# Expert gate and up products of a routed feed-forward layer: one float32 product against three float32r products of halves made on chip

## The reference

```
logits = jnp.einsum('bsd,ed->bse', x, w_router)          # 8 experts
top_vals, top_idx = jax.lax.top_k(logits, 2)
rw = jax.nn.softmax(top_vals, axis=-1)
gate = jnp.einsum('bsd,efd->ebsf', x, w_gate)            # d = 256, f = 512
up = jnp.einsum('bsd,efd->ebsf', x, w_up)
h = jax.nn.silu(gate) * up
y = jnp.einsum('ebsf,edf->bsed', h, w_down)
out = sum over the two chosen experts of rw * y, then a layer norm
```

## Time and profile before

| what | value |
|---|---|
| three runs | 1172.77, 1178.34 and 1179.01 us, median 1178.34 us |
| the profiled execution | 1180.64 us, of which the span of instructions is 1178.8 us |
| instructions | 20227 |
| busy in the span | TensorE 88%, VectorE 61%, ScalarE 47%, GpSimd 51% |

### The profile page before, as it was taken

The page is one execution under the profiler, slowest core; times in us unless marked ns, Lnnn a source line. Parts: engine busy times, 40 slices in busy tenths (PEclk is TensorE's granted clock), DMA queues, the critical chain, the costliest instruction groups (busy, mean ns, idle before and its releaser), DMA issues.

```text
span 1178.8 us, 20227 instructions
## 1 busy us (share of the span) xinstructions
PE 1033.9 (88%) x5678; PEld 823.7 (70%) x5679; DVE 723.2 (61%) x1870; ACT 559.0 (47%) x1201; POOL 604.3 (51%) x662
## 2 busy tenths in 40 slices
PE   5878999999999999995997892799999999999920
PEld 4668999999999999984565662356666666666610
DVE  3766888888888888986778974122222222222237
ACT  1446877887788776651534540122222222222223
POOL 4524776687668767776145666133333333333346
PEclk8979999999999999997978965799999999999965
DMA  9442001001000000111534523122222222222263
GB/s 273 130 116 83 1 3 63 1 1 38 27 1 2 11 1 10 55 55 50 199 119 166 163 55 97 37 45 45 45 45 45 45 45 45 45 44 45 45 144 124
DMA packets 54737, 75.43 MB, mean 64 GB/s; under 512 B 9349, under 2 KB 46979, under 8 KB 52613
## 3 DMA queue, kind: packets, MB, share of 16 engines
q1 hardware_dynamic: 32392, 48.80, 13.3%
q0 software_dynamic: 16640, 18.50, 9.4%
q10 hardware_dynamic: 5628, 7.22, 2.2%
HBM read 45.35 MB, written 29.11 MB: 63 GB/s over the span
## 4 chain that ended last, share of the span: by engine, by line
PE 78%; DVE 6%; issue 5%; DMA 5%; SPq 2%; ACT 2%; POOL 2%; DVEq 0%; POOLq 0%; ACTq 0%
PE bank L1410 19%; PE bank L1149 17%; PE bank L1214 9%; PE bank L1426 9%; PE bank L1209 3%; PE bank L1418 2%; PE bank L1309 2%; PE bank L1119 2%; DMA arena_b<-in_patches 2%; PE bank L1197 2%; PE bank L1177 1%; PE bank L1185 1%; PE bank L1198 1%; SPq L504 1%; PE bank L1312 1%
## 5 line engine op out<-in xcount | busy, mean ns | idle before, releaser
L1077 POOL DMA_INDIRECT yrows<-arena_b,dest_i x64 | 99.8, 1559 | 270.7 <-ACT arena_b L900 258.8
L1410 PE MATMUL bank<-arena_a,arena_b 128*128 x512 | 235.6, 603 | 0.9 <-ACT arena_b L888 0.6
L1559 DVE SCALAR_TENSOR_TENSOR arena_b<-bank,sml,arena_b 128x304 f32<-128x304 f32 (+2 forms) x384 | 195.4, 522 | 23.5 <-ACT arena_b L732 20.3
L1886 DVE TENSOR_TENSOR arena_b<-bank,arena_b 128x512 f32<-128x512 f32 x64 | 44.2, 691 | 200.8 <-PE bank L1410 200.8
L1149 PE MATMUL bank<-xt_hi,w_hi 128*128 128x308 f32 x512 | 160.2, 313 | 1.8 <-DVE arena_b L1559 1.3
L1410 PEld LDWEIGHTS bank<-arena_a,arena_b 128*128 128x128 f32 x512 | 93.0, 192 | 98.4 <-issue 94.7
L1149 PE MATMUL bank<-xt_hi,w_lo 128*128 128x308 f32 x512 | 157.7, 308 | 0.0
L1149 PE MATMUL bank<-xt_lo,w_hi 128*128 128x308 f32 x512 | 156.9, 306 | 0.0
L979 POOL TENSOR_TENSOR u_halves<-arena_b,u_halves 128x308 fp32r<-128x308 f32 x128 | 110.1, 867 | 37.6 <-ACT arena_b L744 37.5
L973 POOL TENSOR_TENSOR y_lo<-arena_b,y_hi 128x308 fp32r<-128x308 f32 x128 | 108.1, 857 | 31.5 <-ACT y_hi L756 31.2
L1426 PE MATMUL bank<-arena_a,arena_b 128*128 x512 | 121.3, 380 | 1.4 <-DVE arena_b L1898 0.9
(11 more groups left out here) (179 smaller groups left out, 2210.4 us busy)
## 6 DMA issues: line engine op xcount, KB each, us to landing
arena_b<-xrows SPq DMA_DIRECT2D x64, 129.0 KB
arena_a<-in_w_gate SPq DMA_DIRECT2D x4, 1024.0 KB
arena_a<-in_w_up SPq DMA_DIRECT2D x4, 1024.0 KB
arena_a<-in_w_down SPq DMA_DIRECT2D x4, 1024.0 KB
yrows<-arena_b SPq DMA_DIRECT2D x1, 3648.0 KB, 18.6
h_all<-seq SPq DMA_DIRECT2D x8, 448.0 KB
w_raw<-in_w_in SPq DMA_DIRECT2D x3, 1024.0 KB
arena_a<-yrows SPq DMA_DIRECT2D x4, 448.0 KB
```

Source lines behind the costliest of these rows:

```text
L1077: pool.indirect_dma_start(yrows, bass.IndirectOffsetOnAxis(ap=dest_i[:, k:k + 1], axis=0), f_y[k], None, compute_op=ALU.add).then_inc(y_se ...
L1410: mm = pe.matmul(bank[q][:, :], x_gt[k][:, d, :], w[:, d, bass.ds(e * FFN, FFN)], start=(d == 0), stop=(d == DC - 1))
L1559: dve.scalar_tensor_tensor(acc[:, :, back_:TXT], x[:, :, 0:TXT - back_], conv_w(s // GROUPS, c, tap), acc[:, :, back_:TXT], ALU.mult, ALU. ...
```

## The change

The gate and up products are taken from halves. ScalarE makes the upper halves of the gate and up weights of block j+1's expert (`upper_weights`, two copies of 128x1024), VectorE the lower halves (`lower_weights`, two subtractions of 128x1024), both in the step of block j. The rows get halves too: ScalarE's copy out of bank 2 now writes `x_hi`, and VectorE subtracts it from bank 2 into `x_lo` (`lower_rows`, 128x256). TensorE then runs twelve float32r matmuls of 512 columns where four float32 matmuls were. ScalarE and VectorE read `expert_i` themselves; TensorE reads it in `down` alone. The two halves of each kind have two buffers, which lie over text memory that is free by then, and over `padbuf`; so ScalarE waits for the sends out of `padbuf` before its first copy. The last norm's small tensors move to another tile, with no other change.

```diff
             def turn(j, k):
                 act.wait_ge(f_tr, j + 1)
                 wait(act, f_um, j - 1)
-                act.activation(x_gt[k], bank[2][...], ACT.Copy).then_inc(f_trc, 1)
+                wait(act, f_xlo, j - 1)
+                act.activation(x_hi[k][:, :, :], bank[2][...], ACT.Copy).then_inc(f_trc, 1)
+            def upper_weights(j, k):
+                e = act.value_load(expert_i[0:1, bass.ds(j, 1)], min_val=0, max_val=EXPERTS - 1)
+                wait(act, f_um, j - 1)
+                wait(act, f_wul, j - 1)
+                act.activation(wg_hi[k][:, :, :], wg_s[:, :, bass.ds(e * FFN, FFN)], ACT.Copy).then_inc(f_wg, 1)
+                act.activation(wu_hi[k][:, :, :], wu_s[:, :, bass.ds(e * FFN, FFN)], ACT.Copy).then_inc(f_wu, 1)
             def expert_step(j, k):
+                upper_weights(j + 1, 1 - k)
                 gate(j)
                 turn(j + 1, 1 - k)
                 back_half(j - 1, 1 - k)
...
             def gate_up(j, k):
-                e = pe.value_load(expert_i[0:1, bass.ds(j, 1)], min_val=0, max_val=EXPERTS - 1)
-                pe.wait_ge(f_trc, j + 1)
-                for q, w, sig, free in ((0, wg_s, f_gm, f_silu), (1, wu_s, f_um, f_hh)):
+                pe.wait_ge(f_xlo, j + 1)
+                for q, hi, lo, ready, sig, free in ((0, wg_hi, wg_lo, f_wgl, f_gm, f_silu), (1, wu_hi, wu_lo, f_wul, f_um, f_hh)):
+                    pe.wait_ge(ready, j + 1)
                     wait(pe, free, j)
-                    for d in range(DC):
-                        mm = pe.matmul(bank[q][:, :], x_gt[k][:, d, :], w[:, d, bass.ds(e * FFN, FFN)], ...)
+                    pairs = [(x, w, d) for d in range(DC) for x, w in ((x_hi, hi), (x_hi, lo), (x_lo, hi))]
+                    for n_, (x, w, d) in enumerate(pairs):
+                        mm = pe.matmul(bank[q][:, :], x[k][:, d, :], w[k][:, d, :], ...)
                     mm.then_inc(sig, 1)
...
+            def lower_weights(j, k):
+                e = dve.value_load(expert_i[0:1, bass.ds(j, 1)], min_val=0, max_val=EXPERTS - 1)
+                dve.wait_ge(f_wg, j + 1)
+                wait(dve, f_um, j - 1)
+                dve.tensor_tensor(wg_lo[k][:, :, :], wg_s[:, :, bass.ds(e * FFN, FFN)], wg_hi[k][:, :, :].bitcast(F32), ALU.subtract)\
+                    .then_inc(f_wgl, 1)
+                dve.wait_ge(f_wu, j + 1)
+                dve.tensor_tensor(wu_lo[k][:, :, :], wu_s[:, :, bass.ds(e * FFN, FFN)], wu_hi[k][:, :, :].bitcast(F32), ALU.subtract)\
+                    .then_inc(f_wul, 1)
+            def lower_rows(j, k):
+                dve.wait_ge(f_trc, j + 1)
+                wait(dve, f_um, j - 1)
+                dve.tensor_tensor(x_lo[k][:, :, :], bank[2][...], x_hi[k][:, :, :].bitcast(F32), ALU.subtract).then_inc(f_xlo, 1)
+            def expert_step(j, k):
+                lower_weights(j + 1, 1 - k)
+                hidden(j, k)
+                lower_rows(j + 1, 1 - k)
+                destinations(j, k)
+                hidden_turned(j, k)
```

More of the change, by code:

```diff
@@ L218, in build, with expert_sb @@
         at = [0]
+        EXPERT_COLS = 2 * ROW + 4 * FFN + 2 * D + GB * 6 + GROUPS * GB * 6
+        with ExitStack() as expert_memory:
+            def expert_sb(name, shape, dt=F32R):
+                return expert_memory.enter_context(nc.sbuf_tensor(name, shape, dt))
+            expert_b = expert_sb("expert_b", [P, EXPERT_COLS], F32)
+            x_hi, x_lo, wg_hi, wg_lo = ([expert_sb(f"{name}{k}", [P, DC, cols]) for k in range(2)]
+                                        for name, cols in (("x_hi", P), ("x_lo", P), ("wg_hi", FFN), ("wg_lo", FFN)))
+            wu_hi = [expert_sb("wu_hi0", [P, DC, FFN])]
+        assert EXPERT_COLS + 4 * DC * P + 5 * DC * FFN <= 9856
         arena_b = sb("arena_b", [P, 9856])
@@ L295, in build @@
         h_all = sb("h_all", [SEQ, BATCH, D])
+        with ExitStack() as expert_memory:
+            wu_hi.append(expert_sb("wu_hi1", [P, DC, FFN]))
+            wu_lo = [expert_sb(f"wu_lo{k}", [P, DC, FFN]) for k in range(2)]
+        assert 3 * DC * FFN <= (EXPERTS + SPARE) * ROW
         padbuf = sb("padbuf", [P, EXPERTS + SPARE, ROW])
@@ L377, in build @@
         at[0] = 0
[L378 to L383, removed]
+        x_g = [part(expert_b, ROW) for _ in range(2)]
+        f_sg = part(expert_b, FFN)
+        f_h = part(expert_b, FFN)
+        f_ht = [part(expert_b, FFN).rearrange("p (c t) -> p c t", c=FC) for _ in range(2)]
+        f_y = [part(expert_b, D) for _ in range(2)]
         at[0] = 0
@@ L387, in build @@
         assert at[0] <= (DC * FFN * 2 + FC * D) * EXPERTS
[L388 to L391, removed]
+        at[0] = 2 * ROW + 4 * FFN + 2 * D
+        y_st = part(expert_b, GB * 6, rows=SEQ).rearrange("p (k s) -> p k s", k=GB)
+        y_mv = [part(expert_b, GB * 2, rows=SEQ).rearrange("p (k s) -> p k s", k=GB) for _ in range(GROUPS)]
+        y_rs = [part(expert_b, GB * 4, rows=SEQ).rearrange("p (s k) -> p s k", s=4) for _ in range(GROUPS)]
         bank = [ctx.enter_context(nc.psum_tensor(f"bank{k}", [P, 512], F32)) for k in range(8)]
@@ L887, in turn @@
                 wait(act, f_um, j - 1)
-                act.activation(x_gt[k], bank[2][:, 0:DC * P].rearrange("p (c t) -> p c t", c=DC), ACT.Copy)\
+                wait(act, f_xlo, j - 1)
+                act.activation(x_hi[k][:, :, :], bank[2][:, 0:DC * P].rearrange("p (c t) -> p c t", c=DC), ACT.Copy)\
                     .then_inc(f_trc, 1)
@@ L905, in expert_step @@
                 back_half(j - 1, 1 - k)
+            act.wait_ge(ld_ffn, 16 * len(FFN_PIECES))
             act.wait_ge(tbl_ready, 2)
+            act.wait_ge(pad_sent, 16 * EXPERTS)
+            act.wait_ge(spare_sent, 16)
+            for k in range(len(x_sent)):
+                act.wait_ge(x_sent[k], 16 * 2 * GB * (GROUPS // len(x_sent)))
+            upper_weights(0, 0)
             turn(0, 0)
+            upper_weights(1, 1)
             gate(0)
@@ L1398, in turn_block @@
                 pe.wait_ge(x_in[k], turn_ * 16 + 16)
-                wait(pe, f_trc, j)
+                wait(pe, f_xlo, j)
                 for d in range(DC):
@@ L1898, in hidden_turned @@
                 dve.tensor_copy(f_ht[k], bank[3][:, :].rearrange("p (c t) -> p c t", c=FC)).then_inc(f_htc, 1)
[L1900 to L1908, removed]
+            def expert_step(j, k):
[4 more added lines that the diff above has]
+                hidden_turned(j, k)
+            lower_weights(0, 0)
+            lower_rows(0, 0)
+            expert_step(0, 0)
+            expert_step(1, 1)
+            expert_step(2, 0)
+            with dve.Fori(1, BLOCKS // 2 - 1) as pair:
+                expert_step(pair * 2 + 1, 1)
+                expert_step(pair * 2 + 2, 0)
+            hidden(BLOCKS - 1, 1)
+            destinations(BLOCKS - 1, 1)
+            hidden_turned(BLOCKS - 1, 1)
             def row_gain(g):
```

7 lines of the change are left out of this document (5 added, 2 removed).

## The result

The changed kernel takes 1219.11 us in the median of 4 runs (1218.34 to 1228.22), beside 1178.38 (1172.77 to 1179.01, 4 runs) before: a ratio of 1.035, 95% interval 1.0306 to 1.0394. It is slower; 1162 had been forecast, with a range that ended at 1179. The profiled execution took 1218.34 us, its span is 1216.3 (1178.8 before).

What follows compares the result with a forecast made beforehand. TensorE was taken to bound the expert stage at 11.79 us per pair of blocks. The new chain of 10.69 plus 0.56 for GpSimd's block gave 11.25, saving 17 us over 32 pairs: 1162 us, 80% range 1137 to 1179.

Steps and rivals of the forecast that it cites:

- the rows come late: Rival, 0.10: SyncE's row load arrives at 3.5 us where TensorE wants it at 3.2; pair 11.55 us, kernel 1170.
- TensorE's saving: Gate and up product: twelve float32r matmuls at 0.228 us take 2.74 us instead of 3.44, 45 us for 64 blocks.
- The chain over both halves of the weights: From one turn_hidden to that two blocks later, through copy back, weight copies, subtractions and hidden: 10.69 us a pair.
- A block by GpSimd: add_bias falls between VectorE's two weight subtractions and delays the second by 0.56 us once a pair, giving 11.25 us.
- No block by GpSimd: Rival, 0.22: lower up weights start before GpSimd asks, or VectorE wins the turn; 10.69 us a pair, 1143 us.
- TensorE stays the bound: Rival, 0.10: the chain is shorter by 0.3 us too; 45 us less, 1133 us, or 1123 with the quicker matmul.
- ScalarE reads only after its copy back: Rival, 0.12: ScalarE reads the expert's number once its copy back has ended; 0.47 more, pair 11.72 us, 1176 us.
- Slower, by the indirect DMA: Rival, 0.08: the indirect DMA holds up VectorE's two-input subtraction, 0.77 us more per chain; pair 12.02 us, 1186 us.
- GpSimd's own queue is no bound: On GpSimd, two unhindered sends start 4.62 us apart, below half the 11.25 us pair, so its queue sets no pace.
- The start adds nothing: At the stage's start, first weights are made while rows load; first product starts 0.8 us later, shorter by as much.
- the tests that the prediction named for itself: Wrong signs: no TensorE idle before turn_hidden, subtractions all alike, row wait before turn_block, clock below 1.00; expected pair 11.25 us.

Runs made afterwards that it cites:

- with the rows ahead: Changed kernel with four row buffers instead of two, SyncE loading rows four blocks ahead: 1178.4 us, ratio 0.9987.
- Without GpSimd and without late rows: Changed kernel with four row buffers, rows loaded four blocks ahead, and add_bias put behind the even block's send and both subtractions: 1144.77 us, ratio 0.9704.
- the run without add_bias: Changed kernel with add_bias on GpSimd dropped, so the last norm's bias is left out of the output: 1179.72 us, ratio 1.0007.
- the kernel before with the rows ahead: Kernel before the change with four row buffers and SyncE loading four blocks ahead: 1176.04 us, ratio 0.9971.
- the changed kernel with the early register load: Changed kernel with TensorE loading the number of down's expert before turn_block's wait for the row block: 1195.57 us, ratio 1.013.
- each alone: Changed kernel with one edit: rows loaded four blocks ahead in four buffers (1178.4 us), or add_bias put behind the even block's send and both subtractions (1178.52 us).
- only both: Changed kernel with four row buffers, rows four blocks ahead, and add_bias behind the even block's send and both subtractions: 1144.77 us, ratio 0.9704.
- the kernel with add_bias moved: Changed kernel with add_bias put behind the even block's send and both weight subtractions, output complete: 1178.52 us, ratio 0.9998.

## Why the prediction was wrong

The step that failed is that the forecast kept the row load off its chain. It stands in the prediction as the rival "the rows come late", at 0.10 and with a price of 0.3 us a pair on top of the forecast's chain. It came true, and it cost 1.41 us. Its arithmetic on the lateness itself was roughly right: 3.5 us against 3.2 from the start of `turn_hidden`, where 3.80 (909.37 to 913.17) stand against 3.25 (909.22 to 912.47 with the rows ahead). The load was taken at 2.2 us and lands after 2.5. What it left out is larger, and it is what stands behind the late instruction: `turn_block`'s wait holds TensorE's queue, in which `down`'s register load comes next, so `down` starts 0.78 us later than behind a punctual `turn_block` (1.00 against 0.22) and takes 0.10 longer to its copy back (2.03 against 1.93). 0.56 + 0.78 + 0.10 = 1.44 on this pair, beside the 1.41 of the mean. The forecast had costed what the change moved on VectorE and ScalarE, and not who is queued behind the wait that it made.

By the prediction's other steps:

- *TensorE's saving*: right. In the changed trace float32r matmuls of 512 columns, ten starts apart from 903.40 to 905.70 us, start 0.230 apart (forecast 0.228), and TensorE alone needs 10.31 us a pair (10.39). The rule that the prediction quotes from the Trainium skill (TensorE: Matmul & The Clock Gate, Back-to-back issue gap) is given there for a matmul by itself and not for a stream of them; its 0.216 us is below the measured 0.230.
- *The chain over both halves of the weights*: right. Without GpSimd and without late rows it is 10.85 us (10.69). From copy back to upper weights it is 1.16 us where 0.90 was taken (902.93 to 904.09), from `hidden` to `turn_hidden` 0.74, as forecast. The 1.16 stands on the block at which ScalarE's loop branches; on the other it is 0.78 (908.22 to 909.00).
- *A block by GpSimd*: the place and the mechanism were right, once a pair on the same block; its size was off. It costs 11.87 - 10.85 = 1.02 us, not 0.56. The forecast charged the second subtraction alone and scaled it from 308 columns; the trace shows both longer, 1.67 and 1.74 in place of 1.23.
- *No block by GpSimd*, *TensorE stays the bound*, *ScalarE reads only after its copy back*: not so. The last comes nearest, since the stretch with ScalarE's load did take 0.26 more than was taken, but its price was 0.47.
- *Slower, by the indirect DMA*: the right side for the wrong reason. The send left the subtractions alone, at 1.23 us, in the run without add_bias.
- *GpSimd's own queue is no bound*: right.
- *The start adds nothing*: right. From the first `turn_block` to the first copy back it is 14.5 us (737.22 to 751.71), where it was 14.7 (743.43 to 758.10). The stage began 6.4 us earlier, which is not of the change: in the kernel before with the rows ahead the first copy back stands at 751.3 as well, and in the changed kernel with the early register load at 760.2.

Together: 10.69 forecast for the chain, + 0.16, + 1.02 for the block, + 1.41 for the rows = 13.28 us a pair. Over 32 pairs, 13.28 - 11.25 = 2.03 would be 65 us more than was forecast, 1227; the first two pairs took only 11.6 us each, one took 2.4 more, the stage began earlier, and 1219 was measured.

Of the tests that the prediction named for itself, three spoke against it: a wait for the rows stood ahead of `turn_block`, the pair between products was 13.3 us in place of 11.25, and TensorE's wait before `turn_hidden` was 1.3 us on one block only, larger than the 0.9 forecast. The granted clock fell below 1.00 as well, on one pair.

What stays open is what it is in a send that goes with a slower row load, and why a late `down` takes 0.10 us longer to its copy back.

## What to carry over

When a bound gets faster, list every transfer and register load that it covered, and follow the new waits round until they close: a late input costs what is queued behind its wait, here 0.88 us on top of 0.56, and 0.9 on top of 0.15. When two costs lie on one chain, one edit shows only its own: here each alone left the kernel at 1178 us, and only both showed that the changed arithmetic is worth 34 us. Small instructions that release a transfer (two 0.14 us copies, a register load) belong ahead of long ones: it costs these about 0.1 us and gave back 24 and 36.

## What the chip showed that was not expected

- add_bias on 114x256 takes 0.72 us when nothing else runs on GpSimd, 1.30 in the kernel before, where its record begins 1.01 us into a send that takes 1.56 (so 0.55 is the send's rest), and 2.38 in the changed kernel. VectorE's two subtractions beside it take 0.44 and 0.51 us longer. By the Trainium skill (SBUF — State Buffer, Who interferes with whom) the later one waits for the whole of the earlier; the trace agrees as far as that the GpSimd instruction and the second subtraction each wait, but by that rule the first subtraction would keep its 1.23 us, and it took 1.67; what makes it longer no run here shows. The rows of the kernel with add_bias moved, by line:

```profile
L1112 POOL TENSOR_TENSOR h_all<-h_all,arena_a x26: 719/722/726, 782.8 to 1079.6; 114x256 f32 x26
```

- Reading an expert's number into a register is dear in its surroundings, not in itself: 0.28 us for the load, but 0.78 from the start of the copy back to the start of the next copy, and 1.16 where the loop's branch lies between them too; the copy back itself takes 0.47. With the load ahead of the copy back this is 0.37 on every block. Together with TensorE's early load it was worth 8 us in the kernel (1144.77 to 1136.47).
